# Adding weighted expert rows into two buffers in memory, and moving the shared expert beside the laying out of tokens

## The chip, the cores and the metric

The kernel runs on one core of a Trainium2 chip. The metric is device time in microseconds of one execution, the median of several runs. Engines: TensorE (PE, its weight loads PEld), VectorE (DVE), ScalarE (ACT), GpSimd (POOL) and SyncE (SP), which issues the direct DMAs. GpSimd issues the indirect ones, whose row numbers are read from an index tensor.

## The reference

One decoder block on x of shape (4, 512, 512) in float32: causal self attention with 16 heads, a cross attention over 1601 context rows, and a feed-forward with 16 experts, each followed by a residual add and a layer norm. The changed code is the feed-forward:

```python
logits = x @ gate_w.T                                  # 2048 tokens x 16 experts
scores = sigmoid(logits)
_, topk_idx = top_k(scores + expert_bias, 4)
topk_w = take_along_axis(scores, topk_idx)
topk_w = topk_w / sum(topk_w)
combine = zeros((T, E)).at[arange(T)[:, None], topk_idx].set(topk_w)
# for each expert e, with ffn(x, wg, wu, wd) = (silu(x @ wg.T) * (x @ wu.T)) @ wd.T
acc = acc + combine[:, e, None] * ffn(x, w_gate[e], w_up[e], w_down[e])
out = layernorm(x + acc + ffn(x, sw_gate, sw_up, sw_down))   # the last one is the shared expert
```

The hidden width is 512, an expert's inner width 256.

## The kernel before

Names: `P` = 128 partitions; `B` = 4 batches of `T` = 512 tokens; `NT` = 16 token tiles of 128, `TT` = 4 in a batch; `DC` = 4 chunks of the 512 features; `IC` = 2 chunks of the inner width; `SLOTS` = 256 rows of an expert tile in `HALVES` = 2 halves; `TILES` = 47, the most tiles that 8192 token-expert pairs can need when every expert starts a new tile. Products are made of a high and a low part of each operand (`hi` by ScalarE as a rounding copy, `lo` by a subtraction), with three matmuls for each product (`PASSES`). Each stage is one `nc.Block()`; all engines meet at its end. Inside a block each engine has its own list of instructions, written out by hand, and semaphores between the lists.

Behind the two attentions three blocks follow.

`route` (L1046) finishes the norm of `rows` (the token rows, kept on chip), stores them to `x2_rows` in memory (L1121), and turns each batch (`turn`, L1305), makes the 16 logits (`logit`, L1316) and their sigmoid (L1163). Then `choose()` finds four experts per token, `rank()` (L1337) counts by matmuls the tokens before each one, and `lay_out()` (L1227) gives each token-expert pair a slot in a row of expert tiles and each tile its expert (`ended`, `expert_at`). For each of 16 token tiles `mark(t)` makes one-hot tables on VectorE (L1279), ScalarE scales them with the token number (L1172), and four matmuls (L1357) sum up which token stands in each slot (`token_at`). Last comes `weigh()`.

`routed_experts` (L1376) loops over the 47 tiles, always all of them. For tile n SP loads the expert's gate, up and down weights, 0.5 MB each, two to three tiles ahead (L1450); GpSimd gathers 2 x 128 token rows from `x2_rows`, three tiles ahead (L1493), when VectorE has written the index (L1560). TensorE does, in one step, the gate product of tile n + 1, the transposes of tile n + 2 (L1621), the up product of tile n + 1 and the down product of tile n. ScalarE reads out the first half (L1541), VectorE the second (L1590), and SP stores 256 rows to `y_rows` (L1470). The buffers of weights, rows and results are doubled, by the tile's parity.

`combine` (L1654) does the shared expert for all tokens: turn again (L1828), gate and up (L1845), down (L1859), in batches of 512. Meanwhile GpSimd gathers for each token tile the four result rows of its tokens (64 gathers, L1707), and VectorE multiplies them with the weights and adds them to `rows` (64 operations, L1772), adds the shared result (L1783), and makes the statistics of the last norm (L600 to L632); ScalarE applies it (L644) and SP stores the output (L1691).

## Time and profile before

| | |
|---|---|
| median of 3 runs | 1556.15 us (1553.42 to 1558.72) |
| the profiled execution's own time | 1543.42 us |
| its span, first to last instruction | 1541.7 us |
| mean granted TensorE clock | 0.943 |
| busy in the span: PE, DVE, ACT, POOL | 1375.3, 1017.8, 789.6, 340.5 us |
| routing's last score transpose to the start of the next block | 917.1 to 956.2 us |
| tile loop, from the start of its block to the last read-out | 956.2 to 1410.8 us |
| behind it, to the end | 130.9 us |

The stretches are stages: each engine's share means something only inside one of them. The granted clock is a part of full speed (2.4 GHz), so that 0.5 is 1.2 GHz. The profiled execution is a little shorter than the median; differences that are worked out in its span are carried over in proportion.

### The profile page before, as it was taken

To read this page: it belongs to the slowest core of one execution; us is meant where nothing else is said; L and a number is where in the kernel's file an instruction comes from. 1 tells how busy PE (TensorE), PEld (TensorE's weight loads), DVE (VectorE), ACT (ScalarE), POOL (GpSimd) and SP (SyncE) were. 2 spreads that over 40 slices of the span, in tenths; PEclk is the share of its full clock that TensorE was granted. 3 is DMA by queue.
4 is the path that set the end of the run, shared out by engine and by line. 5 is a ranking of instruction groups with operands and counts; after the bars stand their busy time and mean duration, and the time that the engine had idled before them with its cause. 6 is when DMAs were issued, how large, how long until landed. Compare 5 with 4: busy or idle time off the path is not lost. (4 is left out here: it accounts for less than half of the span.)

```text
span 1541.7 us, 25128 instructions
## 1 busy us (share of the span) xinstructions
PE 1375.3 (89%) x8837; PEld 1148.1 (74%) x8837; DVE 1017.8 (66%) x1685; ACT 789.6 (51%) x1545; POOL 340.5 (22%) x490
## 2 busy tenths in 40 slices
PE   5899999999998589999999865899999999998990
PEld 5667766766774378888888654899999999997770
DVE  6667676676675564646554378677777777773777
ACT  4777577577576242424233242566566656653222
POOL 0243233234222210100100001222222222222662
PEclk9999999999998789999999985899999999998995
DMA  4200000000000240413220040777788778884563
GB/s 177 110 1 28 1 1 29 1 1 1 1 1 1 87 149 1 128 43 107 65 84 25 2 150 10 270 280 278 287 289 286 273 283 280 284 282 148 168 189 138
DMA packets 62029, 190.37 MB, mean 123 GB/s; under 512 B 7161, under 2 KB 7165, under 8 KB 61185
## 3 DMA queue, kind: packets, MB, share of 16 engines
q1 hardware_dynamic: 49312, 147.93, 26.6%
q0 software_dynamic: 12640, 41.43, 9.0%
q8 instruction: 48, 0.79, 0.2%
q14 instruction: 29, 0.23, 0.0%
HBM read 156.30 MB, written 33.03 MB: 123 GB/s over the span
## 5 line engine op out<-in xcount | busy, mean ns | idle before, releaser
L436 PE MATMUL proj_ps<-wqkv,x_sp 128*128 128x384 f32 x768 | 172.9, 355 | 10.2 <-DVE wqkv L315 10.2
L1549 DVE TENSOR_TENSOR e_w_sp<-e_w_raw,e_w_sp 128x1024 fp32r<-128x1024 f32 x141 | 168.8, 1222 | 18.2 <-ACT e_w_sp L1507 11.5
L1493 POOL DMA_INDIRECT e_x_g<-x_rows,e_index x94 | 101.6, 1080 | 323.0 <-DVE e_index L1560 308.4
L1006 PE MATMUL c_score_ps<-ct,x_t 128*128 128x402 f32 x768 | 160.1, 361 | 0.0
L1507 ACT ACTIVATE e_w_sp<-e_w_raw 128x1024 fp32r<-128x1024 f32 x141 | 145.6, 1058 | 16.1 <-DMA e_w_raw<-w_experts 15.8
L1025 PE MATMUL c_out_ps<-cr,weigh_t 128*128 128x512 f32 (+1 forms) x624 | 147.3, 394 | 1.4 <-DVE weigh_t L865 1.4
L1006 PEld LDWEIGHTS c_score_ps<-ct,x_t 128*128 128x128 f32 x768 | 141.4, 194 | 7.2 <-issue 5.3
L1608 PEld LDWEIGHTS e_gate_ps<-e_x_t,e_w_sp 128*128 128x128 f32 x1128 | 140.5, 191 | 5.9 <-DVE e_x_t L1570 1.8
L1608 PE MATMUL e_gate_ps<-e_x_t,e_w_sp 128*128 128x256 f32 x1128 | 142.1, 282 | 1.4 <-DVE e_x_t L1570 1.4
L1608 PE MATMUL e_up_ps<-e_x_t,e_w_sp 128*128 128x256 f32 x1128 | 143.3, 283 | 0.0
L436 PEld LDWEIGHTS proj_ps<-wqkv,x_sp 128*128 128x128 f32 x768 | 131.7, 194 | 11.6 <-issue 10.1
L1634 PE MATMUL e_down_ps<-e_w_sp,e_h_sp 128*128 128x512 f32 x564 | 139.0, 396 | 0.0
L207 POOL TENSOR_SCALAR_AFFINE_SELECT p_t<-p_t 128x128 f32<-128x128 f32 x256 | 87.3, 353 | 219.8 <-ACT p_t L292 216.0
L1025 PEld LDWEIGHTS c_out_ps<-cr,weigh_t 128*128 128x128 f32 (+1 forms) x624 | 116.1, 188 | 26.2 <-issue 1.7
L1608 PEld LDWEIGHTS e_up_ps<-e_x_t,e_w_sp 128*128 128x128 f32 x1128 | 135.0, 188 | 0.0
L292 ACT ACTIVATE p_t<-score_ps 128x512 f32<-128x512 f32 (+3 forms) x256 | 101.5, 435 | 47.5 <-PE score_ps L492 44.6
L1634 PEld LDWEIGHTS e_down_ps<-e_w_sp,e_h_sp 128*128 128x128 f32 x564 | 102.5, 188 | 21.4
L270 ACT ACTIVATE score_ps<-score_ps,neg_row_max 128x128 f32<-128x128 f32 (+3 forms) x176 | 86.7, 493 | 35.5 <-DVE neg_row_max L388 34.6
L388 DVE TENSOR_REDUCE neg_row_max<-score_ps 128x1 f32<-128x128 f32 (+3 forms) x176 | 82.5, 484 | 29.4 <-PE score_ps L478 27.7
L806 ACT ACTIVATE weigh_t<-c_turn_ps 128x512 fp32r<-128x512 f32 x64 | 31.3, 514 | 136.1 <-PE c_turn_ps L981 136.1
L492 PE MATMUL score_ps<-q_st,k_st 128*128 128x256 f32 (+2 forms) x256 | 86.3, 396 | 13.7 <-ACT p_t L292 12.7
L492 PEld LDWEIGHTS score_ps<-q_st,k_st 128*128 128x128 f32 x256 | 42.6, 191 | 72.9 <-ACT p_t L292 53.7
(212 smaller groups left out, 2377.5 us busy)
## 6 DMA issues: line engine op xcount, KB each, us to landing
e_w_raw<-w_experts SPq DMA_DIRECT2D x141, 512.0 KB, 5.6
y_rows<-e_y SPq DMA_DIRECT2D x47, 512.0 KB
raw<-ctxT SPq DMA_DIRECT2D x16, 800.5 KB, 4.3
raw<-ctx_rows SPq DMA_DIRECT2D x16, 768.0 KB, 4.8
rows<-x_rows SPq DMA_DIRECT2D x1, 4096.0 KB, 12.2
x_rows<-rows SPq DMA_DIRECT2D x4, 1024.0 KB, 5.9
out<-rows SPq DMA_DIRECT2D x4, 1024.0 KB, 5.2
rows<-wqkvT SPq DMA_DIRECT2D x4, 768.0 KB, 7.4
```

Source lines behind the costliest of these rows:

```text
L207: nc.gpsimd.affine_select(out=block_of, in_=block_of, compare_op=ALU.is_ge, fill=0.0, base=0, pattern=[[1, P]], channel_multiplier=-1).the ...
L270: nc.scalar.activation(row_place(n)[:, 0:w], row_place(n)[:, 0:w], ACT.Exp, bias=neg_row_max[:, qt, h:h + 1], accum_out=row_sum[:, qt, h:h ...
L292: nc.scalar.activation(p_t[:, h, p_at[kc]:p_at[kc] + w], score_ps[:, n % 2, kc * P:T], ACT.Exp).then_inc(exped, 1)
L436: mm = nc.tensor.matmul(proj_ps[:, tt, 0:GW], x_sp[:, xs, c, tt * P:(tt + 1) * P], wqkv[:, ws, c, hg * GW:(hg + 1) * GW], start=(c == 0 an ...
L492: nc.tensor.matmul(score_ps[:, n % 2, q0:T], k_st[:, h, kc * P:(kc + 1) * P], q_st[:, h, q0:T], start=True, stop=True).then_inc(scored_t, 1)
L1006: mm = nc.tensor.matmul(score_ps[:, f, 0:MQ], x1_t[:, xs, c, qt * P:(qt + 1) * P], ct[:, cs, c, f * MQ:(f + 1) * MQ], start=False, stop=(c ...
L1025: mm = nc.tensor.matmul(out_ps[:, n % 2, :], weigh_t[0:k, ws, c, :], cr[0:k, cs, c, :], start=(c == 0 and m == 0), stop=(c == MC - 1 and m ...
L1493: nc.gpsimd.indirect_dma_start(x_g[:, par, half, :], None, x2_rows, bass.IndirectOffsetOnAxis(ap=index[:, par, half:half + 1], axis=0)).th ...
L1507: nc.scalar.activation(w_sp[:, par, part, 0, :], w_raw[:, par, part, :], ACT.Copy).then_inc(w_hi[part], 1)
L1549: nc.vector.tensor_tensor(w_sp[:, par, part, 1, :], w_raw[:, par, part, :], w_sp[:, par, part, 0, :].bitcast(F32), ALU.subtract).then_inc( ...
L1608: mm = nc.tensor.matmul(ps[:, par, i, :], w_sp[:, par, part, ws, at:at + P], x_t[:, par, xs, c, :], start=(c == 0 and n == 0), stop=(c == ...
L1634: mm = nc.tensor.matmul(down_ps[:, half, :], h_sp[:, par, hs, i, half * P:(half + 1) * P], w_sp[:, par, DOWN, ws, i * D:(i + 1) * D], star ...
```

## The change

1. The shared expert moves from `combine` into `route`. It uses the turned rows that the logits needed (`x2_t` now keeps all four batches), the PSUM banks of the turns, logits and scores, and lies between ranking and the marks. The low parts of the shared weights and of its hidden values are made by GpSimd. Its result is added to `rows`, and those are stored to the memory buffer `acc[0]`; `acc[1]` is filled with zeros.
2. The weights of a token's experts are stored in 16 more columns of `x2_rows`, so that the gather brings them along (2112 bytes a row instead of 2048). In the tile loop VectorE picks the tile's expert from them (two small operations), and the two read-outs of the result multiply with the weight.
3. Instead of the store to `y_rows`, GpSimd issues for each tile two indirect DMAs that add the 128 rows to the rows of their tokens in memory, in `acc[0]` for even tiles and `acc[1]` for odd ones. Before tile n's the one of tile n - 2 must have landed. Rows of empty slots go to 256 spare rows.
4. The loads of weights get a condition, `fresh_at`: 0 where the tile two before has the same expert, so that its weights are in the same buffer. Rounding and low parts are still made for each tile.
5. `finish_rows` takes the place of `combine`: it loads both buffers, adds them and makes the last norm.

The diff, cut to its core:

```diff
 def route(...):   # SP
+                sp.dma_start(w_raw[:, :, :].rearrange("p a n -> p (a n)"), shared).then_inc(shared_in, 16)
+                sp.dma_start(acc[1][0:NT * P, :].rearrange("(t p) d -> p t d", p=P),
+                             nothing.unsqueeze(1).broadcast_to([P, NT, D])).then_inc(zeros_out, 16)
...
+                sp.wait_ge(weighed, 1)
+                sp.dma_start(x2_rows[0:NT * P, D:D + E].rearrange("(t p) e -> p t e", p=P), weight_row[:, :, :]
+                             ).then_inc(weights_out, 16)
+                for b in range(B):
+                    sp.wait_ge(shared_added, b * TT + TT)
+                    sp.dma_start(acc[0][b * T:(b + 1) * T, :].rearrange("(t p) d -> p t d", p=P),
+                                 rows[:, b * TT:(b + 1) * TT, :]).then_inc(acc_out, 16)
 # GpSimd
+                for part in range(3):
+                    pool.wait_ge(shared_hi, part + 1)
+                    nc.gpsimd.tensor_tensor(w_sp[:, 1, part, :], w_raw[:, part, :], w_sp[:, 0, part, :].bitcast(F32),
+                                            ALU.subtract).then_inc(shared_lo, 1)
+                for b in range(B):
+                    pool.wait_ge(h_hi, b + 1)
...
+                    nc.gpsimd.tensor_tensor(h_sp[:, b % 2, 1, :, :], h_f[:, :, :],
+                                            h_sp[:, b % 2, 0, :, :].bitcast(F32), ALU.subtract).then_inc(h_lo, 1)
 # ScalarE, behind the scores
+                silu(0)
+                hi_h(0)
+                silu(1)
+                columns(0, BEFORE_ADDS)                  # BEFORE_ADDS = 2
+                hi_h(1)
+                columns(BEFORE_ADDS, BEHIND_UP - 4)      # BEHIND_UP = 14
+                silu(2)
+                columns(BEHIND_UP - 4, BEHIND_UP)
+                hi_h(2)
+                columns(BEHIND_UP, NT)
                 act.wait_ge(placed, NT)
+                nc.scalar.activation(token_at[:, 0, :], token_ps[:, 0:2 * TILES], ACT.Copy).then_inc(tokens_out, 1)
+                silu(3)
+                hi_h(3)
 # VectorE
                 choose()
+                gate_up(0)
                 lay_out()
+                for t in range(BEFORE_ADDS):
                     mark(t)
+                gate_up(1)
                 weigh()
+                for t in range(TT):
+                    mark(BEFORE_ADDS + t)
+                    add_shared(t)
+                for t in range(BEFORE_ADDS + TT, BEHIND_UP):
+                    mark(t)
+                gate_up(2)
+                for t in range(BEHIND_UP, NT):
+                    mark(t)
+                    add_shared(TT + t - BEHIND_UP)
+                name_experts()
+                for t in range(TT + NT - BEHIND_UP, 2 * TT):
+                    add_shared(t)
+                find_rows()
+                gate_up(3)
+                for t in range(2 * TT, NT):
+                    add_shared(t)
 # TensorE; front(b, part, first_mark, marks) is 24 matmuls, back(b, first_mark, marks) 4 x 6, with marks between
+                front(0, 0)
+                front(0, 1)
                 rank()
+                front(1, 0)
+                front(1, 1)
+                for t in range(BEFORE_ADDS):
                     mark(t)
+                back(0, BEFORE_ADDS, TT)
+                front(2, 0, BEFORE_ADDS + TT, 2)
+                front(2, 1, BEFORE_ADDS + TT + 4, 2)
+                back(1, BEHIND_UP, NT - BEHIND_UP)
+                front(3, 0)
+                front(3, 1)
+                back(2)
+                back(3)
 def routed_experts(...):   # SP
                     sp.dma_start(w_raw[:, par, part, :],
                                  w_experts[bass.ds(expert, 1), :, part * PART:(part + 1) * PART]
-                                 .rearrange("o p n -> p (o n)")).then_inc(w_in[part][par], 16)
+                                 .rearrange("o p n -> p (o n)"), cond=fresh).then_inc(w_in[part][par], 16)
...
-                        sp.dma_start(dst.rearrange("(h p) d -> p h d", p=P), y[:, par, :, :]
-                                     ).then_inc(y_stored[par], 16)
 # GpSimd, behind the gather of tile n + 3
+                    for half, read in ((0, y_first), (1, y_second)):
+                        pool.wait_ge(consts, 2)
+                        if half == 0:
+                            if past(n, 2):
+                                pool.wait_ge(*earlier)          # the scatters of tile n - 2 have landed
+                            pool.wait_ge(aimed, ready)
+                        pool.wait_ge(read, ready)
+                        nc.gpsimd.indirect_dma_start(
+                            acc[par], bass.IndirectOffsetOnAxis(ap=to_row[:, par, half:half + 1], axis=0),
+                            y[:, par, half, :], None, compute_op=ALU.add
+                        ).then_inc(y_added[par], 16)
 # VectorE, at the start of a step, for tile n + 1
+                    nc.vector.tensor_tensor(weight_in[:, par, :, :], x_g[:, par, :, D:D + E],
+                                            expert_hot[:, bass.ds(m, 1), :].broadcast_to([P, HALVES, E]),
+                                            ALU.mult).then_inc(weight_set, 1)
+                    dve.wait_ge(weight_set, m + 1)
+                    nc.vector.tensor_reduce(weight[:, par, :], weight_in[:, par, :, :], AX, ALU.add
+                                            ).then_inc(weighed, 1)
 # VectorE, at its end, for tile n (ScalarE's read-out of the first half is changed in the same way)
+                        nc.vector.tensor_scalar(to_row[:, par, :], token_at[:, 1, bass.ds(n * HALVES, HALVES)],
+                                                1.0, None, ALU.mult).then_inc(aimed, 1)
-                        nc.vector.tensor_scalar(y[:, par, 1, :], down_ps[:, 1, :], 1.0, None, ALU.mult
+                        nc.vector.tensor_scalar(y[:, par, 1, :], down_ps[:, 1, :], weight[:, par, 1:2], None, ALU.mult
                                                 ).then_inc(y_second, 1)
+def finish_rows(nc, sem, rows, acc, out):
+                for b in range(B):          # SP
+                    for dst, src in ((rows, acc[0]), (odd_rows, acc[1])):
+                        sp.dma_start(dst[:, b * TT:(b + 1) * TT, :],
+                                     src[b * T:(b + 1) * T, :].rearrange("(t p) d -> p t d", p=P)
+                                     ).then_inc(row_in[b], 16)
+                for b in range(B):          # VectorE
+                    dve.wait_ge(row_in[b], 32)
+                    for t in range(b * TT, (b + 1) * TT):
+                        nc.vector.tensor_tensor(rows[:, t, :], rows[:, t, :], odd_rows[:, t, :], ALU.add
+                                                ).then_inc(summed, 1)
+                    for t in range(b * TT, (b + 1) * TT):
+                        dve.wait_ge(summed, t + 1)
+                        gather(t)           # the statistics of tile t
+                    aggregate(dve, b)
+                    normalise(dve, b)
```

## Rows read from the trace of the kernel before

**Rows 1.** The page's first line.

```profile
span 1541.7 us, 25128 instructions
```

**Rows 2.** Busy time by stretches: us, busy us of each engine (instructions), granted clock, DMA.

```profile
918.00:956.00 38.00, 19.38 (x97) 17.03 (x97) 34.71 (x116) 11.96 (x18) 0.00 (x0) 0.52 0.00 0
...
1100.00:1200.00 100.00, 100.00 (x737) 94.22 (x736) 74.73 (x98) 61.99 (x88) 23.98 (x22) 1.00 0.80 280
...
1465.00:1541.70 76.70, 35.01 (x155) 27.32 (x154) 56.66 (x108) 19.88 (x27) 32.88 (x32) 0.77 0.52 164
```

**Rows 3.** Groups of instructions from 940 us on: busy us, mean ns, idle before.

```profile
L1772 DVE SCALAR_TENSOR_TENSOR rows<-y_g,weight_of,rows 128x512 f32<-128x512 f32 x64 | 43.0, 747 | 0.0
...
L1845 PE MATMUL s_gate_ps<-s_x_t,shared_sp 128*128 128x512 f32 x96 | 25.3, 422 | 4.2 <-DVE s_x_t L1747 4.2
...
L1756 DVE TENSOR_TENSOR s_h_f<-s_up_ps,s_gated 128x1024 f32<-128x1024 f32 x4 | 4.9, 1224 | 3.5 <-issue 2.5 <-ACT s_gated L1724 1.0
...
L613 ACT ACT_TABLE_LOAD x2 | 2.6, 1283 | 17.5 <-DVE norm_mean_var L607 17.5
```

**Rows 4.** Timeline of routing: TensorE, VectorE, GpSimd; start, duration, idle before.

```profile
916.42 0.66 PE L1333 MATMUL r_score_ps<-r_ident,logits_t 128*128 128x128 f32 x4 [0.69 <-ACT logits_t L1161]
925.46 0.20 PE L1342 MATMUL r_rank_ps<-chosen_b,earlier 128*128 128x16 bf16 x1 [8.38 <-DVE scan L1231]
...
937.32 17.00 PE L1357 MATMUL r_token_ps<-col_hot,row_hot 128*128 128x94 f32 x64 [9.43 <-ACT col_hot L1172]
...
927.93 0.29 DVE L1233 TENSOR_TENSOR filled<-r_rank_ps,steps_of 128x128 f32<-128x128 f32 x1 [2.47 <-PE r_rank_ps L1348]
...
929.42 0.94 DVE L1247 TENSOR_TENSOR ended<-count,scan 128x752 f32<-128x752 f32 x1
...
935.38 0.69 DVE L1279 TENSOR_TENSOR row_hot<-count,low_f 128x512 fp32r<-128x512 f32 x1
...
956.19 0.20 POOL L1480 MEMSET e_ident<- 128x128 f32 x1 [72.01 <-POOLq L1111]
```

**Rows 5.** Timeline of one steady tile: TensorE, VectorE, GpSimd.

```profile
1206.46 1.04 PE L1621 MATMUL e_turn_ps<-e_ident,e_x_g 128*128 128x128 f32 x8
...
1215.75 1.03 PE L1621 MATMUL e_turn_ps<-e_ident,e_x_g 128*128 128x128 f32 x8
...
1204.57 0.17 DVE L1560 TENSOR_SCALAR e_index<-token_at 128x2 uint32 x1
...
1205.49 1.20 POOL L1493 DMA_INDIRECT e_x_g<-x_rows,e_index  x1 [6.86 <-DVE e_index L1560]
1206.99 0.95 POOL L1493 DMA_INDIRECT e_x_g<-x_rows,e_index  x1 [0.30 <-issue]
```

**Rows 6.** Timeline behind the last tile: TensorE, VectorE, ScalarE.

```profile
1494.92 8.67 PE L1859 MATMUL s_down_ps<-shared_sp,s_h_sp 128*128 128x512 f32 x36 [1.52 <-DVE rows L1783]
...
1410.07 0.69 DVE L1590 TENSOR_SCALAR e_y<-e_down_ps 128x512 f32<-128x512 f32 x1 [2.11 <-PE e_down_ps L1634]
...
1529.87 2.47 DVE L600 BATCH_NORM_STATS2 norm_stats<-rows 128x6 f32<-128x512 f32 x4
...
1534.04 2.92 ACT L644 ACTIVATE rows<-rows,norm_half_v,norm_rstd 128x512 f32<-128x512 f32 x4 [1.03 <-DVE norm_half_v L632]
```

**Rows 7.** DMA queues from 1200 to 1300 us, and landing of all gathers of L1493.

```profile
q1 hardware_dynamic: 7623, 22.60, 60.8%
q0 software_dynamic: 1755, 5.75, 18.5%
...
DMA to landing us min/median/max: 3.8/6.0/8.1
```

**Rows 8.** DMA issues of the page: count, KB each, us to landing.

```profile
rows<-x_rows SPq DMA_DIRECT2D x1, 4096.0 KB, 12.2
...
out<-rows SPq DMA_DIRECT2D x4, 1024.0 KB, 5.2
```

**Rows 9.** GpSimd's subtract of 512 elements in self attention.

```profile
L196 POOL TENSOR_TENSOR qk_sp<-qk_cos,qk_sp 128x512 fp32r<-128x512 f32 x16 | 20.4, 1274 | 22.1 <-ACT qk_sp L247 22.1
```

504 lines of the change are left out of this document (218 added, 286 removed).

## The prediction

> **What bounds the kernel now.** I read the page's first lines, then the busy time of each engine by stretches, then the timeline of each engine in three places: the end of routing, one steady tile, and everything behind the last tile. The span is 1541.7 us, the execution's own time 1543.4; the median of three runs is 1556.15, so the sum below is made in the span and carried over as a ratio [rows 1].
>
> The tile loop is bound by TensorE: from 1100 to 1200 us it is busy 100.00 of 100 us at granted clock 1.00, VectorE 74.73, ScalarE 61.99, GpSimd 23.98, the DMA engines 80% [rows 2]. One tile takes 1215.75 - 1206.46 = 9.29 us [rows 5]. So in the loop only what makes TensorE wait counts. On both sides of it TensorE is not the bound. From 918 to 956 us it is half idle at granted clock 0.52 (close to 1.2 of 2.4 GHz); from 1465 to the end it is busy 35 of 77 us and VectorE 57 [rows 2]. That is where work can move.
>
> **The tail: what goes.** The last tile's second half is read out at 1410.07 + 0.69 = 1410.8. Everything behind it (shared expert, 64 gathers, 64 weighted adds, last norm) takes 1541.7 - 1410.8 = 130.9 us [rows 6]. It goes altogether: 64 gathers, 64 adds of 747 ns and 288 matmuls [rows 3]. In its place:
> - The last scatter must land. Its issue starts about 0.75 us behind the read-out, as the gather at 1205.49 does behind the index op that ends at 1204.74 [rows 5], and a gather takes a median 6.0 us to land [rows 7]: 7 us (before it was 1414.0 - 1410.8 = 3.2).
> - Two loads of 1 MB before the first batch can be summed. 1 MB lands in 5.2 us and 4 MB in 12.2 [rows 8], so each MB more costs 2.3 and the fixed part is 2.9: 2.9 + 2 x 2.3 = 7.5. Later pairs come each 4.7 us, with a 1 MB output store among them 7.0.
> - Per batch VectorE does four adds, 43.0 / 64 = 0.67 us each where they follow one another [rows 3] = 2.7, and statistics to shift, 1529.87 to 1534.0 = 4.1 [rows 6]: 6.8 us, level with the transfers. The first pays a table load of 1.3 [rows 3]. Behind the last adds comes what stands behind 1529.87 now: 1541.7 - 1529.9 = 11.8 [rows 6].
> Sum: 7 + 7.5 + 1.3 + 3 x 6.8 + 2.7 + 11.8 = 50.7; I take 51. Bounds 47 (scatter lands in 3.8, a little less per batch) to 58 (every store delays a pair by its 2.3). **Term: -80.**
>
> **Routing: what is added.** The chain is TensorE's, with the new waits laid in. At full clock 36 matmuls of this width take 8.67 us [rows 6], so the 24 of a shared half 5.7, the six of a down projection 1.4; all 288 (three groups of 96, as the gate's [rows 3]) 69.4.
> - The last score transpose ends at 917.1 [rows 4]. Gate and up of batch 0 follow at once: 928.5. In the kernel before TensorE sits idle for 8.4 us there, until `choose()` is done at 925.4 [rows 4], so of 11.4 us only 3.1 are new. The rank matmuls, 2.5 us now at the lower clock (VectorE idles 2.47 for them), take 1.4: 929.9. With no gap I expect the granted clock to stay at its upper level.
> - Gate and up of batch 1: 941.3. Beside them VectorE does the product of batch 0 (1.22), the layout (927.93 to 935.38 = 7.5, less 2.0 for naming the experts, two ops of 0.94 and small ones, which moves behind the marks) and two marks of 1.06 (16 in 17.00): 937.6, hidden [rows 3, 4].
> - Back of batch 0 with marks 2 to 5 between its tiles. VectorE has the product of batch 1 (to 942.6), the four steps of weighing (1.5), then per tile a mark 1.06 and an add 0.67; a mark goes through ScalarE (0.6) before TensorE. VectorE, ScalarE and TensorE hand over to each other: about 2.0 per tile, 952.4.
> - Front of batch 2 with eight marks: 11.4 + 8 x 0.4 = 14.6, 967. VectorE waits at the product of batch 2 before marks 14 and 15, so back of batch 1 is again paced by hand-overs: 974. Naming the experts (2.8) lies beside it.
> - Front of batch 3: 985.6. Back of batches 2 and 3: VectorE's adds of batch 2 stand behind the product of batch 3; eight tiles of 1.4: 997. Last add 997.6.
> - GpSimd makes the low halves: a 512-element subtract costs it 1.27 us [rows 9], so 1024 cost 2.5. The three for the weights lie under the logits. The four for the hidden halves run beside VectorE's marks, which read two SBUF operands. The trace before has no such pair; bounds are nothing and 2.5 us for each of the three that have no slack. I take 3: 1000.6.
> - SP stores the summed rows and the block waits: the 1 MB store, 5.2 us [rows 8]: 1006. The other additions to SP (zeros 4 MB, about 12 us by the 4 MB row; a weight column store) land long before.
> The stage ended at 956.2 [rows 4]. **Term: +50**, bounds +44 (no blocking, quicker hand-overs) and +60 (each blocked, hand-overs a half longer).
> The Trainium skill, "SBUF — State Buffer", section "Who interferes with whom", says that a VectorE instruction with two SBUF inputs and a GpSimd one that reads SBUF exclude each other for a whole instruction. By that rule the term would be +54 instead of +50; with no such lock, +47. No row here shows it.
>
> **The tile loop.** VectorE gets three small ops (two for the weight, ahead of the gather's index; one for the target index) of 0.17 each, 0.5 us; its idle per tile is 2.3, and they stand before waits on ScalarE and TensorE [rows 2, 5]: nothing. Without that cover they would cost 0.5 x 47 = 24. The scale on ScalarE rides on the copy: nothing. Skipped loads: computing the reference's routing on its inputs fills 40 of the 47 tiles, and only 25 tiles have another expert than the tile two before, so 22 x 1.5 MB aren't read. As TensorE never waited for a weight, that gives nothing directly; it frees DMA time. SP loses the store and its wait for both read-outs and gets two reads of the plan more; its loads go out no later.
> GpSimd gets two scatters more, and they stand ahead of the next gather: the second scatter waits for the read-out just before the index op at 1204.57. So two issues (0.95 to 1.20 each and 0.3 between, [rows 5]) start about 1203.9 and 1205.3, and the gathers at 1206.6 and 1208.0 instead of 1205.49 and 1206.99. The transpose that reads them is at 1215.75 [rows 5]. The second gather had 8.8 us to land and gets 7.7; median 6.0, longest 8.1 [rows 7]. Late is then `turn`, behind it gate, up and back of the tile. The read-outs and the scatter also wait for the scatter of two tiles before: 18.6 us for a landing of 6 to 8, nothing.
> DMA time: in 100 us the hardware queue used 60.8% for 22.60 MB, GpSimd's 18.5% for 5.75 [rows 7]. The y store is 5.77 of the 22.60: 15.5%. An accumulating scatter costs at least what a gather of the same bytes does (18.5%), and, taken as a gather plus a store of the row, 34%. The whole: 79.3 - 15.5 + 18.5 = 82%, or 98%, on a tile that loads weights; 45.3% less on one that doesn't. I take the upper price. It fits, barely, in runs of loading tiles (tiles 14 to 26, 11 of 13 load), so landings lengthen. I allow 0.25 us for each of the 25: **term +6**, bounds 0 and +30.
> The Trainium skill, "Collectives: The Full Stack", section "The bandwidth ceiling: the fold count and why AG ≠ RS ≠ AR", says an add inside a DMA halves the rate, since two sources are read. By that rule the scatter takes 31 to 37%, and the allowance stays.
>
> **Sum:** -80 + 50 + 6 = -24 on 1541.7, ratio 0.9844; 1556.15 x 0.9844 = 1532 us. A change under 0.3% (5 us) can't be told from none here.
>
> **Rivals.**
> 1. *Forecast*, 1532, own range 1518 to 1546. Chance 0.60.
> 2. *Late gathers (other side).* Place: `turn` in the tile loop, behind scatters on GpSimd's queue. If an accumulating row costs a gather and two stores, the loading tile needs 98 + 15.5 = 113% of the engines, 1.2 us over the 9.29, and with it, I estimate, 0.6 for landings that lengthen: 1.8 us on each of 25 tiles, 45 us; -30 + 45 = +15, 1571. It decides from 30 us, 1.2 on a loading tile. For it: one queue for both, 1.1 us of slack gone. Against: 22 tiles without loads. Chance 0.17.
> 3. *Accumulation is slow row by row.* If rows are taken one after another, the quickest landing of a gather, 3.8 us for 8 rows an engine [rows 7], gives 0.48 a row; read and write 0.95, 16 rows an engine and tile: 15.2 us against 9.29, +277 us, -30 + 277 = +247: 1805. Chance 0.08.
> 4. *Routing takes back nearly all.* TensorE falls to the lower clock in some of its waits or hand-overs are dearer: +20 more, 1552 (1542 to 1562). Chance 0.10.
> 5. *More is gained*: no stall, route +44, tail 47: -84 + 44 = -40, 1516. Chance 0.05.
> Faster: 0.60 + 0.05 + half of 4 = 0.70. Same: most of the other half and the edge of 2, 0.06. Slower: the rest, 0.24. The range 1514 to 1575 leaves out case 3, the upper part of 2 and half of 5.
>
> **What would show it.** Route's block ends near 1006; TensorE has no gap over 2 us between 917 and 997 and granted clock near 1.0. Tile pitch 9.29, the transposes' wait for x in sum under 10 us. From last read-out to end 51 us, of which VectorE some 27. The prediction is wrong if TensorE waits for `e_x_g` on most tiles, if DVE or ACT wait for the scatter of two tiles before, or if the marks take over 1.5 us each beside GpSimd.

## The result, and the profile after

The changed kernel takes 1544.23 us (median of 4 runs, 1543.19 to 1545.83), the kernel before 1555.33 in the same comparison (4 runs): ratio 0.9927, 95% interval 0.9907 to 0.9947. That is faster by 0.7%, where 1.6% was forecast (1532 us, ratio 0.9844); it lies in the range of 1514 to 1575.

The page's first line of the changed kernel, and its busy time by the stretches that answer to those of [rows 2] (columns as there):

```profile
span 1542.1 us, 25698 instructions
```

```profile
918.00:1006.00 88.00, 78.62 (x391) 63.72 (x389) 56.95 (x140) 20.24 (x28) 10.08 (x5) 0.98 0.11 38
1100.00:1200.00 100.00, 96.12 (x688) 89.63 (x687) 75.65 (x121) 58.72 (x82) 62.22 (x41) 1.00 0.87 219
1490.00:1542.10 52.10, 0.00 (x0) 0.00 (x0) 24.38 (x73) 14.19 (x21) 1.49 (x1) 0.50 0.74 254
```

The columns are the stretch, its length, busy us (and instructions) of TensorE, its weight loads, VectorE, ScalarE and GpSimd, the granted clock, the DMA share and GB/s. Routing has become a TensorE stage at full clock (78.62 of 88 us busy, granted clock 0.98, where it had been half busy at 0.52). The tail has no TensorE work left. And in the tile loop, where TensorE was busy 100.00 of 100 us, it now is 96.12: something makes it wait. GpSimd went from 23.98 to 62.22.

The two spans are equal (1541.7 and 1542.1), yet the runs differ by 11 us. The profiled execution of the kernel before was itself some 12 us quicker than its runs. Two later profiles of it, unchanged, had spans of 1550.2 and 1556.6. I use the first of these, e0, as the measure of "before"; its own time was 1552.0 us, some 3 below the median of 1555.33. Each part runs between marks that both kernels have: the last score transpose, GpSimd's first memset of the loop, the first transpose of x, the last read-out, the end. In us:

| part | before, first profile | before, e0 | after | after - e0 |
|---|---|---|---|---|
| up to the last score transpose | 917.1 | 914.9 | 919.7 | +4.9 |
| routing, to the block's end | 39.1 | 39.1 | 90.5 | +51.4 |
| to the first transpose of x | 11.8 | 11.7 | 8.9 | -2.8 |
| tile loop, to the last read-out | 442.8 | 441.9 | 468.5 | +26.6 |
| tail | 130.9 | 142.6 | 54.4 | -88.2 |
| span | 1541.7 | 1550.2 | 1542.1 | -8.1 |

The first part holds the same code in both kernels and varied between 914.9 and 919.9 over all profiles.

**Routing** of the changed kernel: timeline of TensorE, VectorE, GpSimd (start, duration, idle before).

```profile
919.46 11.16 PE L1501 MATMUL r_turn_ps<-r_x_t,r_w_sp 128*128 128x512 f32 x48
930.46 0.18 PE L1470 MATMUL r_rank_ps<-chosen_b,earlier 128*128 128x16 bf16 x1
...
949.88 0.62 PE L1485 MATMUL r_token_ps<-col_hot,row_hot 128*128 128x94 f32 x4 [4.55 <-ACT col_hot L1230]
...
932.70 2.89 DVE L1312 TENSOR_TENSOR scan<-scan 128x16 f32<-128x16 f32 x4
...
945.98 2.66 DVE L1361 TENSOR_TENSOR row_hot<-count,low_f 128x512 fp32r<-128x512 f32 x1
...
949.62 0.68 DVE L1361 TENSOR_TENSOR row_hot<-count,low_f 128x512 fp32r<-128x512 f32 x1
...
975.43 2.41 DVE L1361 TENSOR_TENSOR row_hot<-count,low_f 128x512 fp32r<-128x512 f32 x1
...
933.13 2.43 POOL L1181 TENSOR_TENSOR r_h_sp<-r_h_f,r_h_sp 128x1024 fp32r<-128x1024 f32 x1 [14.82 <-ACT r_h_sp L1223]
945.52 2.56 POOL L1181 TENSOR_TENSOR r_h_sp<-r_h_f,r_h_sp 128x1024 fp32r<-128x1024 f32 x1 [9.97 <-ACT r_h_sp L1223]
...
1010.22 0.20 POOL L1662 MEMSET e_ident<- 128x128 f32 x1 [11.81 <-POOLq L1132]
```

The 48 matmuls of a batch's gate and up take 11.16 us and the rank matmuls follow without a gap, as foreseen. One wait is longer than 2 us: 4.55 for a marked column. VectorE's first operation of a mark lasts 2.66 us at 945.98, beside GpSimd's subtract at 945.52, and 0.68 when GpSimd is idle (949.62); at 975.43 it lasts 2.41 beside the subtract at 974.92. Four scans take 2.89 beside the subtract at 933.13, and 0.81 in the kernel before.

**A steady tile** of the changed kernel: timeline of TensorE and GpSimd.

```profile
1192.83 1.09 PE L1845 MATMUL e_turn_ps<-e_ident,e_x_g 128*128 128x128 f32 x8 [0.31 <-DMA e_x_g<-x_rows,e_index]
...
1202.94 1.09 PE L1845 MATMUL e_turn_ps<-e_ident,e_x_g 128*128 128x128 f32 x8 [0.47 <-DMA e_x_g<-x_rows,e_index]
...
1180.56 1.62 POOL L1691 DMA_INDIRECT acc_rows<-e_y,e_to_row  x1 [4.08 <-DVE e_to_row L1810]
1182.49 2.10 POOL L1691 DMA_INDIRECT acc_rows<-e_y,e_to_row  x1 [0.30 <-issue]
1184.89 1.02 POOL L1673 DMA_INDIRECT e_x_g<-x_rows,e_index  x1 [0.30 <-issue]
1186.22 1.56 POOL L1673 DMA_INDIRECT e_x_g<-x_rows,e_index  x1 [0.30 <-issue]
```

Here DMA_INDIRECT from `e_y` to `acc_rows` is the issue of a scatter, and the one from `x_rows` to `e_x_g` that of a gather. The scatters' issues last 1.62 and 2.10 us, not 0.95 to 1.20, so the gathers behind them start 4.3 and 5.7 us after the first scatter's start. The transposes come 10.1 us apart (9.29 in [rows 5]) and wait for x. Over the loop, the waits of TensorE (us in total, times, longest), the queues from 1164 to 1264 us (packets, MB, share of the 16 engines), and GpSimd's issues from 1064 to 1464 us (busy, mean ns):

```profile
PE e_turn_ps L1845 <- DMA e_x_g<-x_rows,e_index: 15.1, 14, 2.0
...
q0 software_dynamic: 4549, 10.76, 52.2%
q1 hardware_dynamic: 3456, 12.58, 38.8%
...
L1691 POOL DMA_INDIRECT acc_rows<-e_y,e_to_row x81 | 152.7, 1885 | 123.3 <-DVE e_to_row L1810 105.8 <-issue 8.5 <-DVE e_index L1783 5.8
L1673 POOL DMA_INDIRECT e_x_g<-x_rows,e_index x82 | 99.9, 1218 | 25.0 <-issue 25.0
```

**The tail** of the changed kernel: timeline of VectorE, GpSimd, SP. The last read-out ends at 1487.67.

```profile
1507.22 2.50 DVE L1912 TENSOR_TENSOR rows<-rows,odd_rows 128x512 f32<-128x512 f32 x4 [19.55 <-DMA odd_rows<-acc_rows]
...
1514.99 2.49 DVE L1912 TENSOR_TENSOR rows<-rows,odd_rows 128x512 f32<-128x512 f32 x4
...
1521.45 2.49 DVE L1912 TENSOR_TENSOR rows<-rows,odd_rows 128x512 f32<-128x512 f32 x4
...
1489.93 1.55 POOL L1691 DMA_INDIRECT acc_rows<-e_y,e_to_row  x1 [0.30 <-issue]
...
1498.96 0.39 SPq L1893 DMA_DIRECT2D rows<-acc_rows  x1
```

The last scatter is issued 2.3 us behind the read-out and the loads begin 9.0 us after it: 11.3. The first pair is there 8.3 later, and a batch then takes 6.46 us on VectorE (1521.45 - 1514.99).

### The profile page after: what moved, and what is told of

Same layout as the page of the kernel before. It is cut to its first block and busy times, and to the rows that moved or that the text cites. A ratio compares the mean times of both kernels' runs of the same rounds, so it can differ in the third digit from the quotient of the medians.

```text
span 1542.1 us, 25698 instructions
## 1 busy us (share of the span) xinstructions
PE 1364.8 (89%) x8773; PEld 1138.9 (74%) x8773; DVE 1000.3 (65%) x1760; ACT 784.7 (51%) x1529; POOL 476.0 (31%) x527
## 3 DMA queue, kind: packets, MB, share of 16 engines
q1 hardware_dynamic: 38352, 108.73, 20.8%
q0 software_dynamic: 21056, 50.07, 16.6%
## 5 line engine op out<-in xcount | busy, mean ns | idle before, releaser
L1691 POOL DMA_INDIRECT acc_rows<-e_y,e_to_row x94 | 174.9, 1861 | 148.7 <-DVE e_to_row L1810 123.9
L1832 PE MATMUL e_up_ps<-e_x_t,e_w_sp 128*128 128x256 f32 x1128 | 147.9, 287 | 0.0
L1832 PEld LDWEIGHTS e_gate_ps<-e_x_t,e_w_sp 128*128 128x128 f32 x1128 | 142.6, 190 | 5.9 <-DVE e_x_t L1791 2.0
L436 PEld LDWEIGHTS proj_ps<-wqkv,x_sp 128*128 128x128 f32 x768 | 131.8, 194 | 11.7 <-issue 10.2
L1832 PEld LDWEIGHTS e_up_ps<-e_x_t,e_w_sp 128*128 128x128 f32 x1128 | 139.4, 190 | 0.0
L1025 PEld LDWEIGHTS c_out_ps<-cr,weigh_t 128*128 128x128 f32 (+1 forms) x624 | 116.1, 188 | 26.2 <-issue 1.7
L1673 POOL DMA_INDIRECT e_x_g<-x_rows,e_index x94 | 113.1, 1203 | 44.0 <-issue 27.7
L806 ACT ACTIVATE weigh_t<-c_turn_ps 128x512 fp32r<-128x512 f32 x64 | 31.3, 515 | 136.3 <-PE c_turn_ps L981 136.3
L492 PE MATMUL score_ps<-q_st,k_st 128*128 128x256 f32 (+2 forms) x256 | 86.6, 397 | 13.7 <-ACT p_t L292 12.6
## 6 DMA issues: line engine op xcount, KB each, us to landing
x_rows<-rows SPq DMA_DIRECT2D x4, 1024.0 KB, 13.7
```

What stands on the lines that cost most here:

```text
L436: mm = nc.tensor.matmul(proj_ps[:, tt, 0:GW], x_sp[:, xs, c, tt * P:(tt + 1) * P], wqkv[:, ws, c, hg * GW:(hg + 1) * GW], start=(c == 0 an ...
L1025: mm = nc.tensor.matmul(out_ps[:, n % 2, :], weigh_t[0:k, ws, c, :], cr[0:k, cs, c, :], start=(c == 0 and m == 0), stop=(c == MC - 1 and m ...
L1673: nc.gpsimd.indirect_dma_start(x_g[:, par, half, :], None, x2_rows, bass.IndirectOffsetOnAxis(ap=index[:, par, half:half + 1], axis=0)).th ...
L1691: nc.gpsimd.indirect_dma_start(acc[par], bass.IndirectOffsetOnAxis(ap=to_row[:, par, half:half + 1], axis=0), y[:, par, half, :], None, co ...
L1832: mm = nc.tensor.matmul(ps[:, par, i, :], w_sp[:, par, part, ws, at:at + P], x_t[:, par, xs, c, :], start=(c == 0 and n == 0), stop=(c == ...
```

## The experiments

Theory: late gathers take the missing gain, because two longer issues and the adding's DMA time stand before them. Rivals: DMA time alone; the order of issues alone; slower matmuls; and something in routing or tail. Each "expected" is the text that stood before the run. Ratios are against runs of the kernel before on the same chip. The loop runs from the first transpose of x to the last read-out, and the waits leave out the one before that first transpose. Loops of the same kernel differed by up to 1.8 us between profiles (before: 441.3 to 442.8; changed: 466.7 and 468.5).

| kernel | us | ratio, 95% interval | loop, us | waits for x, us |
|---|---|---|---|---|
| after | 1544.2 | 0.993, 0.991 to 0.995 | 468.5 | 15.1 |
| e1 gathers first | 1524.4 | 0.980, 0.977 to 0.984 | 450.3 | 0.6 |
| e2 plain scatter | 1521.3 | 0.978, 0.974 to 0.981 | 450.3 | 0.9 |
| e3 every weight loaded | 1562.4 | 1.005, 1.003 to 1.007 | 486.3 | 31.3 |
| e4 padding | 1538.7 | 0.989, 0.985 to 0.992 | 463.2 | 16.4 |
| e5 gathers first, padding | 1519.5 | 0.978, 0.976 to 0.979 | 444.0 | 1.5 |
| e6 gathers first, every weight loaded | 1525.3 | 0.982, 0.980 to 0.984 | 451.2 | 1.8 |
| e7 before, skipping alone | 1555.0 | 1.001, 0.999 to 1.003 | 442.1 | 0 |
| e8 before, shared expert moved | 1568.5 | 1.009, 1.007 to 1.011 | 442.1 | 0 |
| e9 half rows added | 1531.9 | 0.987, 0.986 to 0.989 | 459.0 | 6.5 |

**The order of issues (e1).** In GpSimd's step of tile n, the gathers of tile n + 3 now stand ahead of the scatters of tile n - 1, so the scatters are issued a step later. The lines left out let GpSimd's loop run one step further.

```diff
                 def step(n, par):
                     if exists(n + 3):
                         gather(n + 3, 1 - par)
-                    if exists(n):
-                        scatter(n, par)
+                    if exists(n - 1):
+                        scatter(n - 1, 1 - par)
...
```

> The gathers of the next tile are issued ahead of the scatters of the last one on GpSimd; nothing else changes. Theory order (the gathers come late because two scatter issues of 1.6 to 2.1 us stand ahead of them): TensorE's 15 us of waits at the transposes go, the loop from the first transpose to the last read-out falls from 468.5 us to about 453, the whole from 1544 to about 1529. Theory DMA time (the adding scatters fill the DMA engines, and the gathers share them in any order): at most 5 us less, since the same bytes move in the same period.

Measured: 1524.35 us. TensorE's waits and the queues over the same stretches as above:

```profile
PE e_turn_ps L1852 <- DMA e_x_g<-x_rows,e_index: 0.6, 1, 0.6
...
q0 software_dynamic: 4793, 11.48, 56.2%
q1 hardware_dynamic: 3170, 11.54, 34.0%
```

The software queue takes even more of the engines (56.2%) and x is in time. So DMA time alone does not make x late; it takes the place behind the scatters. The loop shortens by 18.2 us for 14.5 of waits. Most of the difference lies in how a wait is counted. It is counted from the end of the gate matmuls, but without a wait the transposes start 0.16 us ahead of that end (median of 24 tiles of the changed kernel). On the 13 waiting tiles that its timeline resolves, the step from the start of the gate matmuls to that of the up matmuls is 16.6 us longer in all, for 13.7 of recorded waits. By that, the waits explain about 3 of the 3.7 us (an estimate).

**What the adding costs (e2, e9).** e2 drops the adding (rows overwrite each other, the sums are left out); e9 adds half of each row. Its row number counts rows of half the width, so the halves also land closer together, in the first half of the buffer; that was not tested by itself.

```diff
-                            y[:, par, half, :], None, compute_op=ALU.add
+                            y[:, par, half, :], None
```

```diff
-                            acc[par], bass.IndirectOffsetOnAxis(ap=to_row[:, par, half:half + 1], axis=0),
-                            y[:, par, half, :], None, compute_op=ALU.add
+                            acc[par].rearrange("r (h d) -> (r h) d", h=2),
+                            bass.IndirectOffsetOnAxis(ap=to_row[:, par, half:half + 1], axis=0),
+                            y[:, par, half, 0:D // 2], None, compute_op=ALU.add
```

> The scatters overwrite the rows instead of adding to them (so the expert sums are left out and the output is not the sum). Theory DMA time: GpSimd's queue falls from 52% of the engines to about 37%, the waits for x fall below 5 us, the issue of a scatter from 1.86 us to the 1.2 of a gather, whole about 1530. Theory order: the issue is as long as before or a little shorter, gathers stay behind it, waits of 8 us or more remain, whole about 1538.

> The changed kernel with scatters that add 1 KB of each row in place of 2 KB, so half of the weighted results is left out; as many rows, as many scatters, the old order of issues. It separates the two halves of the scatters' cost: the time their issues stand ahead of the gathers on GpSimd (expected the same, 1.6 to 2.1 us a tile and half) and the time they take from the DMA engines (software queue 52% of them after, about 34% expected here). Theory A (DMA time makes x late, the issue time only uses up the slack): waits of TensorE for x under 4 us in all, as with the plain scatters (0.9 us), the whole near 1525 us, ratio 0.982. Theory B (the issues standing ahead make it late): issue stays near 1.86 us, waits stay at 10 us or more, the whole within 4 us of 1544. A third outcome, the issue time itself falling with the bytes to about 1.3 us, would say that the two can't be told apart by size, since the issue is long because the queue's engines are behind.

Measured: 1521.34 and 1531.88 us. First e2, then e9 (waits, queues, issues):

```profile
PE e_turn_ps L1845 <- DMA e_x_g<-x_rows,e_index: 0.9, 1, 0.9
...
q0 software_dynamic: 3440, 11.46, 33.7%
...
L1691 POOL DMA_INDIRECT acc_rows<-e_y,e_to_row x86 | 111.0, 1291 | 177.0 <-DVE e_to_row L1810 156.9 <-issue 13.8 <-DVE e_y L1814 4.4
```

```profile
PE e_turn_ps L1846 <- DMA e_x_g<-x_rows,e_index: 6.5, 9, 1.8
...
q0 software_dynamic: 4642, 8.37, 38.0%
...
L1691 POOL DMA_INDIRECT acc_rows<-e_y,e_to_row x83 | 155.6, 1875 | 112.0 <-DVE e_to_row L1811 93.5 <-issue 9.6 <-DVE e_index L1784 5.8
```

Adding costs twice: the issue on GpSimd is 1885 ns on the mean instead of 1291, and the software queue's share is 56.2% (e1, 11.48 MB) instead of 33.7% (e2, 11.46 MB). Halving the bytes leaves the issue at 1875 ns and takes the share to 38.0%; waits fall from 15.1 to 6.5 us. e2 came out as its theory of DMA time said (waits of 0.9 us, issue near that of a gather), and quicker than the 1530 us expected. e9 lies between its two theories, and neither held alone: more than half of the waiting goes with the bytes, the rest only where the issues too are shorter (e2) or stand behind (e1).

**Skipping loads (e3, e6, e7).** e3 and e6 load every weight again, in the changed kernel and in the one with the gathers first; e7 puts the skipping alone into the kernel before.

```diff
-                                 .rearrange("o p n -> p (o n)"), cond=fresh).then_inc(w_in[part][par], 16)
+                                 .rearrange("o p n -> p (o n)")).then_inc(w_in[part][par], 16)
```

> Every tile loads its weights, as the kernel before did (the condition on the load is taken away). Theory DMA time: tiles without a load gave the engines air; with all 47 loading each tile waits 1 us or more at the transposes or for weights: 20 to 45 us more, whole 1565 to 1590. Theory order: the wait comes from the issue order, so the load changes little: under 8 us more.

> Gathers ahead of the scatters, and every weight loaded again (no load skipped). It tells what the skipping is worth once the order of issues is mended. Theory (waits for x come from issue order and DMA time together): with the order mended and the engines of DMA near 0.9 busy, waits of 0 to 10 us in all instead of 31.3; the whole 1524 to 1534 us, ratio 0.980 to 0.987. Rival (the DMA engines' time alone makes x late, and order only moves slack): waits stay above 20 us, the whole at 1540 to 1555 us. If the waits are nil and the time is that of the gathers first alone, 1524 us, skipping buys nothing in this version.

> The kernel before with one part of the change alone: weights that the buffer already holds are not loaded again. Theory: the loop of the kernel before has no wait of TensorE for x or for weights, so taking DMA work away buys nothing: same within 0.3%, loop 442.8 us within 2. Rival (the DMA engines' load slows it in a way that no wait shows, as the 1.1% between skipping and not skipping after the change would suggest): faster by 0.5 to 1.1%, 1537 to 1546 us.

Measured: 1562.36, 1525.32 and 1555.01 us. e3's waits and queues:

```profile
PE e_turn_ps L1845 <- DMA e_x_g<-x_rows,e_index: 31.3, 22, 2.7
...
q0 software_dynamic: 4323, 10.31, 48.3%
q1 hardware_dynamic: 4181, 15.24, 44.9%
```

In the changed order the skipping is worth 18 us, which is a little less than the 20 to 45 of the theory of DMA time and far more than the 8 of the theory of order; without it the whole change is 0.5% slower than before (ratio 1.005, 1.003 to 1.007). With the gathers first it is worth nothing (1525.3 and 1524.4), and in the kernel before nothing either (ratio 1.0014). It is a cover for the late gathers, not a gain. What is skipped is a little less than predicted: the hardware queue moved 140.19 MB in e3 and 108.73 after the change, and the difference is 60 loads of 0.5 MB, so 20 tiles and not 22.

**Slower matmuls (e4, e5, e10, e11).** After the change the 24 gate matmuls of a tile take longer, and what changed about them is the addresses: the weights' tiles and wider rows of `x_g` now lie ahead of `x_t`. The four kernels shift `x_t` by a tile behind `e_weight`; e4 in the changed kernel, the others with the gathers first. The size is 48 floats in e4 and e5, 64 in e10, 16 in e11.

```diff
         weight = sb("e_weight", [P, 2, HALVES])
+        sb("e_pad", [P, 48])
```

> 192 unused bytes a partition stand ahead of the transposed rows, so that these start at the same place modulo 256 bytes as in the kernel before. Theory placement (the 24 matmuls of a half take 2.88 and 2.95 us instead of 2.81 and 2.89 because of where their operands lie): the pitch of a tile without waits falls from 9.42 to 9.29 us, whole 6 us less. Rival (the slower matmuls come from something else, as DMA traffic or waits in TensorE's list): no change, within 1 us.

> The changed kernel with both repairs at once: the gathers issued ahead of the scatters, and 192 bytes of padding behind the routing weights' tile. Theory (the two losses of the loop are separate: waits for x, and slower gate and up matmuls): the loop gives back both, last read-out 443 to 447 us behind the first transpose, as in the kernel before (442.8), against 468.5 after, 450.3 with the gathers first alone and 463.2 with the padding alone; 24 gate matmuls at 2.80 us; the whole about 1518 us, ratio 0.976. Rival (both edits work through the same thing, the moment at which x is there): nothing on top of the gathers first, 1524 us, ratio 0.980, loop 450.

> Gathers first, with 256 bytes of padding behind the routing weights' tile in place of 192: a control for the padding's gain of 5 to 6 us. Theory (what counts is where the tile of x, the moving operand, starts modulo 256 bytes; a shift by 256 changes nothing): gate matmuls stay at 282 ns and up at 285 ns on the mean, the loop at 450 us, the whole at 1524 us, ratio 0.980. Rival (any shift, or the distance to another tile, does it): 279 and 283 ns, loop 444 us, 1519 us, ratio 0.978.

> Gathers first, with 64 bytes of padding at the same place: the tile of x starts neither where the changed kernel has it nor at a multiple of 256 bytes. If only a start at a multiple of 256 bytes is quick, gate and up stay at 282 and 285 ns and the loop at 450 us (1524 us); if starts at a multiple of 128 bytes are quick too, 279 and 283 ns, loop 444 us (1519 us).

Measured: 1538.70, 1519.53, 1524.76 and 1521.07 us. The gate's group from 1064 to 1364 us (count, busy us, mean ns) in e1, e5, e10, e11:

```profile
L1839 PE MATMUL e_gate_ps<-e_x_t,e_w_sp 128*128 128x256 f32 x768 | 97.2, 282 | 0.0
```

```profile
L1840 PE MATMUL e_gate_ps<-e_x_t,e_w_sp 128*128 128x256 f32 x768 | 94.9, 279 | 0.0
```

```profile
L1840 PE MATMUL e_gate_ps<-e_x_t,e_w_sp 128*128 128x256 f32 x768 | 97.2, 282 | 0.0
```

```profile
L1840 PE MATMUL e_gate_ps<-e_x_t,e_w_sp 128*128 128x256 f32 x768 | 96.0, 281 | 0.0
```

A shift by 256 bytes does nothing (loop 450.6 us), one by 192 restores the rate (444.0), one by 64 gives most of it back in the loop (444.8), though only part in the gate's mean (281 ns). The theory of the place modulo 256 bytes held for e10; that only the multiple of 256 is quick is refuted by e11. The loops differ by more than two profiles of one kernel do, but the shifts by 256 and by 64 bytes have one profile each. Which tile's place counts, `x_t` or one of those shifted with it, was not separated. The two losses add up, as e5 expected: 1544 less 20 less 5.

e5 is the best version found: 1519.5 us, 2.2% below the kernel before on its chip. On the chip of e10 and e11, where the kernel before takes 1541.2 us, these gain 1.1% and 1.3%.

**The parts added up (e8).** The kernel before with the shared expert moved and loads skipped, results still stored by tile and gathered at the end. Beside the lines shown, it has room for the gathered results of eight token tiles in place of four.

```diff
-                pe.wait_ge(consts, 2)
-                for c in range(DC):
-                    turn(0, c)
-                front(0)
...
+                front(0, 0)
+                front(0, 1)
                 rank()
...
```

> The kernel before with the shared expert moved beside the laying out of tokens (and the skipping of loads), but with the results stored by tile and gathered and added at the end as before: no adding scatters. Theory (the parts add up): from last score to the next block 90 us against 39.1, first transpose 3 us sooner behind that, the loop as before, 443 us without waits, and a tail bound by the 64 gathers' issues at about 1.1 us each and the last norm, about 91 us against 130.9: 1553 + 51 - 3 - 40 = 1561 us, ratio 1.005 (1550 to 1572). Rival (the loop suffers by what the route leaves behind, its placement or its buffers, not by the scatters): the loop at 450 us or more and the whole at 1568 or more.

Measured: 1568.49 us: routing 87.3 us, loop 442.1 without waits for x, tail 116.4 against 91 expected. The end of its tail, GpSimd and VectorE:

```profile
1539.81 0.94 POOL L1848 DMA_INDIRECT y_g<-y_rows,slot_of  x1 [0.30 <-issue]
...
1546.08 0.17 DVE L619 TENSOR_SCALAR norm_half_v<-norm_mean_var 128x4 f32<-128x4 f32 x1 [3.32 <-remote]
...
1548.15 10.68 DVE L1868 SCALAR_TENSOR_TENSOR rows<-y_g,weight_of,rows 128x512 f32<-128x512 f32 x16
```

The loop clears the rival: what routing leaves behind doesn't slow it. The changed loop's loss came with what e8 leaves out, the adding scatters and the weights that travel with the rows. The tail missed for two reasons. The 64 issues follow one another from 1458.24 to 1540.75, 1.29 us each instead of the 1.1 priced, so 82.5 us and not 70. And 30 us instead of some 20 stand behind the last one. From 1518.1 to 1534.9 VectorE takes 1.4 us for each add that lasts 0.75, and it stands for 3.32 us before 1546.08; the records name only "issue" (no wait that the profile shows) and "remote" (another core or an unknown queue). So 16 of the 64 adds are still to do at 1548.15, when the gathers' traffic has ended (DMA share 0.00 from 1543 to 1546). What holds VectorE there isn't shown. Its 26.5 us of waits for gathers to land all lie before 1504, while GpSimd issues without a stop, so they set nothing. So the moved expert alone loses (+48.2 in routing, -26.2 in the tail against e0), and only the removal of the gathers (116.4 to 54.4) pays for it.

**The two times of the kernel before (e0, e14, e12, e13).** e0 and e14 are the kernel before, unchanged; e13 the changed kernel; e12 the kernel before with:

```diff
-        RING = 4
+        RING = 2
```

> The kernel before, unchanged, for a second look at its profile. Its first profiled execution lasted 1543.4 us where its runs last 1553.5, and with the skipping of loads added, which moves nothing else, the profiled one lasted 1553.7: there the first 1410 us agree within 3 us and the last part lasts 143.5 us against 130.9. Theory: the kernel before has that longer last part in its usual runs: a span near 1551.9, 143 us from the last read-out to the end, with TensorE idle some 6 us behind the transposes of the shared expert's third batch, for no wait that a record shows. Rival: the skipping of loads causes it, and this look gives 131 us again.

> The kernel before, with room for the gathered results of two token tiles in place of four, so 8 gathers are issued at once behind the tile loop in place of 16. In the second look at the kernel before, TensorE stood still for 7.3 us in the shared expert (from 1425.5 to 1432.9) with no wait in the records, while the 16 first gathers' traffic ran (1411 to 1432), and began again as it ended. Theory (something TensorE needs, its instructions for one, stands behind the gathers' traffic on chips where that happens at all): with traffic that ends some 10 us sooner the standstill ends sooner or is gone, so TensorE's idle time without a wait in that stage falls under 3 us, where the unchanged kernel of the same call shows its 6 to 7. Rival (it is bound to a place in TensorE's program): the standstill stays 6 us or more at the same transposes. The whole time is no test, since a smaller ring also delays later gathers; I expect 1545 to 1560.

> The changed kernel, unchanged, timed again beside the kernel before. The kernel before has lasted 1551 to 1554 us on the median in four calls and 1541 in one, while the kernel with the gathers first was at 1524 in both kinds. Theory: the changed kernel stays at 1543 to 1546 whichever the chip, so its ratio is 0.993 to 0.996 where the kernel before takes 1551 to 1555 and 1.000 to 1.003 where that takes 1541. Rival: the changed kernel is quicker too on such a chip, near 1532, and the ratio stays 0.993.

> The kernel before, unchanged, beside the other two: its profile on this chip. If its runs here are near 1541, its last part takes 131 us and has no standstill of TensorE without a wait; if near 1553, 142 to 144 us, with one of 6 to 7.5 us behind the transposes of the shared expert's third batch.

Measured: 1552.0 (one run), 1568.2, 1543.4 and 1558.4 us (one run). Timeline of TensorE, ScalarE and VectorE in the shared expert, and two stretches of 5 us; first e0, then e12:

```profile
1424.54 1.04 PE L1828 MATMUL s_turn_ps<-s_ident,rows 128*128 128x128 f32 x8
1432.90 1.11 PE L1828 MATMUL s_turn_ps<-s_ident,rows 128*128 128x128 f32 x4 [7.33 <-issue]
...
1431.52 0.60 ACT L1717 ACTIVATE s_x_t<-s_turn_ps 128x512 fp32r<-128x512 f32 x1 [14.91 <-remote]
...
1432.15 0.69 DVE L1747 TENSOR_TENSOR s_x_t<-s_turn_ps,s_x_t 128x512 fp32r<-128x512 f32 x1 [14.81 <-issue]
...
1430.00:1435.00 5.00, 1.11 (x4) 0.71 (x4) 0.70 (x2) 1.24 (x3) 1.06 (x2) 0.58 0.52 147
1435.00:1440.00 5.00, 4.26 (x12) 3.56 (x13) 3.76 (x6) 1.96 (x3) 0.86 (x1) 0.50 0.00 0
```

```profile
1425.87 1.03 PE L1828 MATMUL s_turn_ps<-s_ident,rows 128*128 128x128 f32 x8
1427.88 1.25 PE L1828 MATMUL s_turn_ps<-s_ident,rows 128*128 128x128 f32 x8 [0.98 <-DVE s_x_t L1747]
...
1425.00:1430.00 5.00, 4.02 (x26) 3.20 (x25) 2.09 (x4) 2.52 (x5) 0.00 (x0) 1.00 0.00 0
```

In e0 TensorE stands for 7.33 us, for which its own record names no releaser, and starts again at the lower clock (0.50). The other engines' rows name one: in the program the next transposes wait for VectorE's subtract, which waits for ScalarE's read-out, and here each starts within 0.1 us of the end of the one before (1431.52 + 0.60, 1432.15 + 0.69, 1432.90). So it is ScalarE that comes late. Its read-out starts 6.98 us behind the start of the transposes that it reads, and 0.63 in the first profile of the kernel before (1428.12 and 1428.75) and in e12. e7 and e14 show the same chain, with ScalarE 5.69 and 4.20 us behind and gaps of TensorE of 6.03 and 4.54.

What holds ScalarE isn't shown ("remote"). In these three it goes on 2 to 4 us before the 16 gathers' traffic ends (in e0 at 1431.52, with traffic up to 1433.7), so the standstill does not last as long as the traffic, as the text before e12 took it. e12, with 8 gathers at once, has no such gap there; but that is one profile, and the first profile of the kernel before had none with 16 either. e12 as a whole took 1568.2 us, where 1545 to 1560 was expected. e0 came out as expected (a tail of 142.6 us); e14's tail was 147.4, longer than the 142 to 144 expected, with a second standstill, of VectorE, at 1461.89 (it starts 5.9 us behind the end of the up matmuls that it reads). e14's chip gave the longer time, so the expectation for e13 was tested only there: 1543.4, as before. On the chip of e10 and e11 the kernel before took 1541.2 us (7 runs); the changed kernel was not run on that one.

## Why the prediction was right and wrong

**The step that failed is the tile-loop term**, "I allow 0.25 us for each of the 25: term +6, bounds 0 and +30". It measured +26.6 (+25.7 against the first profile), inside its bounds but over four times the term. The mechanism is that of rival 2, in smaller size: it was priced 45 us and was 15, in 14 waits. What makes the sum up:
- The order of issues, 18.2 us, which e1 gives back: 14.5 of waits for x and, by the estimate at e1, some 3 that come with them. The prediction priced a scatter's issue at 0.95 to 1.20 us "each and 0.3 between", from rows of gathers; adding scatters take 1.62 and 2.10. It had the second gather lose 1.1 us of its 8.8 us of slack; it starts 6.3 us ahead of the transposes' due time (1192.5 - 1186.2), so it loses 2.5.
- Slower matmuls, 6.3 us (450.3 - 444.0): not foreseen at all. The prediction took gate and up as unchanged, but the change moved their operands.
- The rest, 2.1 us (444.0 in e5, 441.9 in e0), of which 1.5 are waits that e5 still has.

**The DMA price held roughly.** I took an adding scatter as 34% of the engines, where a gather takes 18.5%. If in e2 gathers and scatters share the 33.7% evenly, 16.9 each, adding ones take 56.2 - 16.9 = 39%. That is a factor of 2.3; with 18.5 for the gathers it is 15.2 and 37.7, a factor of 2.5. The page "Collectives: The Full Stack" of the Trainium skill, section "The bandwidth ceiling: the fold count and why AG ≠ RS ≠ AR", has a ReduceScatter run at half the rate of an AllGather, since its add reads two sources. It says so of rings between cores; carried over to a scatter, as the prediction did, it would give a factor of 2, and here it is somewhat dearer. That rule says nothing of the issue, which in this kernel counted as well.

**Routing held.** +50 forecast, +51.4 measured, the block's end at 1010.2 instead of 1006, of which 2.6 us were there at the last score transpose (919.7 instead of 917.1). The 3 us taken for GpSimd and VectorE blocking each other were about the right size. Two of the subtracts met a mark that TensorE then waited for, and these marks took 2.0 and 1.7 us longer than the 0.68 of one alone. By the prediction's own signs that was a warning (marks of over 1.5 us, and a wait of TensorE of over 2 us, the 4.55), though the sum held. The page "SBUF — State Buffer", section "Who interferes with whom", of the Trainium skill says such instructions exclude each other; the trace agrees (0.68 us alone, 2.66 beside a subtract). The prediction's "The trace before has no such pair" is wrong. There is one in self attention, beside GpSimd's subtract that runs from 24.23 to 25.49 us; the same operation lasts 0.72 us in the median of its 32:

```profile
24.29 1.75 DVE L335 TENSOR_TENSOR qk_cos<-qk_cos,qk_sin 128x512 f32<-128x512 f32 x1
```

**The tail held as a length, not as a difference.** 51 forecast, 54.4 measured: the last scatter and the start of the loads took 11.3 instead of 7, the first pair 8.3 instead of 7.5, the rest 34.9 instead of 36.2. But what it replaced took 142.6 us in e0 (143.5 in e7, 147.4 in e14), not 130.9: "The tail: what goes" read the one profile in which ScalarE, and with it TensorE, did not stand still. In e0 the matmuls behind the gap are 8.5 us later against the last read-out than in that profile, and 10.6 once TensorE has passed through its slow clock. Carrying the sum over as a ratio assumed that the 13 us between that profile and the runs (1543.4 and 1556.15) would stay in the new kernel; they lay in the tail and went with it. Against e0 the same lengths give -92 + 50 + 6 = -36, a span of 1514, and the measured 1542.1 misses it by 28: 20.6 in the loop, 3.7 in the tail, 4.9 in the unchanged first part, 1.4 in routing, less 2.8 before the first transpose. The forecast missed by 12 only because the ratio hid the rest.

**Skipped loads** gave "nothing directly", as written; indirectly they kept the change from being slower (e3). Of the other signs, VectorE and ScalarE never waited for the scatter of two tiles before, and the pitch of a tile was not 9.29 us even without waits (9.42), which is the matmuls' part.

**What was open and is not settled:** what holds ScalarE, and VectorE in e14 and e8, beside many gathers in some executions and not in others; the change removes those gathers. On a chip where the kernel before takes 1541 us, the changed kernel at 1543 to 1544 would be no gain; that comparison was not run.

## What to carry to other kernels

Before a new transfer is put on a queue that also feeds the bound engine, put the feeding ones first: here that swap was worth 20 us, more than the change itself (11), and made 31 MB of skipped loads unnecessary. Price an operation by its issue on the engine as well as by its traffic, and take both from the same kind of transfer. When an engine stands with no releaser named, follow the other engines' rows back through the program's waits. When one profiled execution differs from the timed runs by as much as the effect in question, find the stage in which it differs before summing against it.

## What the runs showed of the hardware

- An indirect DMA that adds took GpSimd 1.62 to 1.89 us to issue (means of kernels), a plain one 1.29, and half the bytes did not shorten it (1.88).
- Matmuls with the same shapes and counts took 279 or 282 ns (gate, 256 columns) according to where the operands lie: a shift by 192 bytes gave 279, one by 64 281, one by 256 left 282.
- While 16 indirect gathers of 256 KB ran, ScalarE started a read-out 4.2 to 7.0 us behind the start of the transposes it reads, and not 0.63, in three of the four profiles with that order (e0, e7, e14); with 8 it was 0.63 in the one profile. No record names what it lacked. TensorE stood for up to 7.33 us behind it, with its granted clock at 1.00 ahead of that gap and 0.50 behind it.
- VectorE's operation of 0.68 us took 2.66 beside a GpSimd subtract of 2.56.
